# Masked cross attention on one core: one maxima pair in each step, side projections spread over the steps, the sums copied out by ScalarE ahead of the reciprocal

## The reference

```
x = x + L0_xattn(ln(x), ctx)          # cross attention, one head
x = x + L0_attn(ln(x))                # causal self attention, 16 heads
x = x + L0_ffn(ln(x))                 # mixture of 8 experts
x = x + L1_xattn(ln(x), ctx, mask)    # masked cross attention, then self attention, then a gelu layer
x = x + L1_attn(ln(x), key, value)    # quantised self attention
x = x + L1_ffn(ln(x))                 # mixture of 8 experts

# the first part of L1_xattn:
q = split_heads(x @ cq_w + cq_b)      # 16 heads of 8
k = split_heads(ctx @ ck_w + ck_b)
v = split_heads(ctx @ cv_w + cv_b)
scores = einsum('bqhd,bkhd->bhqk', q, k) / sqrt(8) + mask
probs = softmax(scores, axis=-1)      # over the 1601 keys
ca = einsum('bhqk,bkhd->bqhd', probs, v)
```

## Time and profile before

| | |
|---|---|
| median of 3 runs | 1376.42 us (1372.77 to 1376.95) |
| profiled execution | 1376.45 us, its span 1374.6 us |
| PE busy | 1044.6 us (76%) |
| DVE busy | 724.5 us (53%) |
| ACT busy | 489.2 us (36%) |
| POOL busy | 223.0 us (16%) |
| mean granted TensorE clock | 0.881 of full speed |
| masked cross attention | the exponentials begin at 485.2 us, the last starts at 973.1 us |

### The profile page before, as it was taken

The page is one execution under the profiler, slowest core; times in us unless marked ns, Lnnn a source line. Parts: engine busy times, 40 slices in busy tenths (PEclk is TensorE's granted clock), DMA queues, the critical chain, the costliest instruction groups (busy, mean ns, idle before and its releaser), DMA issues.

```text
span 1374.6 us, 22315 instructions
## 1 busy us (share of the span) xinstructions
PE 1044.6 (76%) x9246; PEld 738.4 (54%) x9246; DVE 724.5 (53%) x1194; ACT 489.2 (36%) x633; POOL 223.0 (16%) x202
## 2 busy tenths in 40 slices
PE   3676774998863789999999999998476545729888
PEld 1455453777751356666666666665345323428766
DVE  4234766433443556666666656663376477864121
ACT  0235231222231145555555555555223102403333
POOL 2000423121221001111111111100142004220110
PEclk9899886999995589999999999999888867758999
DMA  8581010010302332222333233320000000010110
GB/s 264 193 342 76 1 43 4 25 45 23 93 0 91 112 117 102 101 100 101 115 132 125 100 109 115 103 73 17 1 1 0 1 0 0 1 31 16 32 37 24
DMA packets 41346, 98.47 MB, mean 72 GB/s; under 512 B 9976, under 2 KB 24960, under 8 KB 41264
## 3 DMA queue, kind: packets, MB, share of 16 engines
q1 hardware_dynamic: 41264, 97.29, 20.9%
HBM read 55.49 MB, written 0.73 MB: 41 GB/s over the span
## 4 chain that ended last, share of the span: by engine, by line
PE 46%; DVE 17%; issue 15%; ACT 11%; POOL 4%; SPq 3%; DMA 3%; DVEq 0%; POOLq 0%
PE PS L262 44%; ACT PT L1084 7%; DVE kl L1475 3%; DVE mx L1492 3%; ACT kh L1071 2%; DVE prT L1481 2%; SPq L893 2%; DVE u_all L275 1%; POOL work_area L390 1%; DMA ctxT<-in_ctx_T 1%; POOL PT L390 1%; DVE x L675 1%; POOL blank_g L257 1%; POOL rstd_all L281 1%; PE PS L292 1%
## 5 line engine op out<-in xcount | busy, mean ns | idle before, releaser
L1492 DVE TENSOR_REDUCE mx<-PS 128x2 f32<-128x1024 f32 x192 | 230.4, 1217 | 74.8 <-PE PS L262 74.6
L1084 ACT ACTIVATE PT<-PS 128x1024 f32<-128x1024 f32 (+1 forms) x208 | 212.4, 1021 | 97.9 <-PE PS L262 97.9
L262 PE MATMUL PS<-QB,KS 128*128 128x256 f32 (+1 forms) x832 | 166.8, 323 | 25.1 <-ACT PT L1084 17.9
L262 PE MATMUL PS<-QB,QS 128*128 128x512 f32 x576 | 159.1, 425 | 24.5 <-DVE wcol L663 22.5
L262 PEld LDWEIGHTS PS<-QB,KS 128*128 128x128 f32 (+1 forms) x832 | 115.7, 187 | 70.2 <-ACT PT L1084 37.6
L262 PEld LDWEIGHTS PS<-QB,QS 128*128 128x128 f32 x576 | 109.7, 201 | 61.5 <-issue 27.6
L262 PE MATMUL PS<-PT,work_area 128*32 128x128 f32 (+1 forms) x3328 | 134.4, 279 | 0.5 <-ACT PT L1084 0.5
L262 PE MATMUL PS<-KS,QB 64*128 64x512 f32 (+1 forms) x512 | 109.7, 459 | 11.5 <-DMA KS<-kl 9.5
L675 DVE SCALAR_TENSOR_TENSOR x<-PS,wcol,x 128x128 f32<-128x128 f32 x128 | 44.9, 350 | 138.1 <-PE PS L262 134.7
L262 PEld LDWEIGHTS PS<-PT,work_area 128*32 128x32 f32 (+1 forms) x3328 | 78.4, 109 | 43.6 <-issue 36.2
L262 PE MATMUL PS<-nat_area,work_area 128*128 128x128 f32 (+2 forms) x928 | 85.0, 275 | 13.7 <-DVE work_area L670 5.9
(11 more groups left out here) (240 smaller groups left out, 1420.1 us busy)
## 6 DMA issues: line engine op xcount, KB each, us to landing
KS<-kh SPq DMA_DIRECT2D x32, 800.5 KB
ctxT<-in_ctx_T SPq DMA_DIRECT2D x24, 800.5 KB, 4.9
nat_area<-in_ctx_tiles SPq DMA_DIRECT2D x16, 832.0 KB, 6.5
KS<-kl SPq DMA_DIRECT2D x16, 800.5 KB
work_area<-in_ctx_T SPq DMA_DIRECT2D x8, 800.5 KB, 10.1
nat_area<-in_L_ffn_experts_w SPq DMA_DIRECT2D x24, 256.0 KB, 3.2
nat_area<-in_L_ffn_W SPq DMA_DIRECT2D x16, 256.0 KB, 3.0
KS<-mask_parts SPq DMA_DIRECT2D x32, 50.1 KB
```

The source lines that it names most:

```text
L262: return T.matmul(o, l, r, start=start, stop=stop, **k)
L1084: P["exp_a"].done(S.activation(PT[0:rows, par, :], PS[0:rows, 1024:2048], ACT.Exp), f"e{k}")
L1492: ins = V.reduce_max(by_pair[:, :, j // 3, j % 3:j % 3 + 1], src, AX)
```

## The change

- **Maxima.** Each of the 13 steps has exactly one maxima item: steps 0 to 9 have m3 to m12 of batch n + 1, steps 10 to 12 have m0 to m2 of batch n + 2. `MAX_STEPS` goes away.
- **Side items.** The key chunks are in steps 0 to 3 (before in 1 to 4), the sum in step 4 (before 5). The value projection is spread by tiles: tiles 0 to 7 two a step over steps 5 to 8, tiles 8 to 11 in step 9, tile 12 in step 11 (before four tiles each in steps 6, 7 and 8 and tile 12 in step 9). ACT empties a group when its last tile is done. nm stays in step 10.
- **Order on PE in a step.** Scores, nm, the maxima item, the side items, then the value product of the step before. DVE takes nm ahead of the step's maxima item.
- **The sum.** ACT copies bank 7 into `rsum`, and DVE takes the reciprocal in place there. PE's wait for bank 7 behind the sum is for ACT's copy (`sum_a`), no longer for the reciprocal (`sum_v`).
- SP's and POOL's programs are not edited.

```diff
+        progress("sum_a", ["sum"])
...
         def maxima(n, k):
-            b = n + 1 if k < 11 else n + 2
-            return [(b, j) for j in MAX_STEPS[k]] if 0 <= b < BATCH else []
+            b, j = (n + 1, k + 3) if k < 10 else (n + 2, k - 10)
+            return [(b, j)] if 0 <= b < BATCH else []
...
+        def value_group(c):
+            return next(g for g, (k0, k) in enumerate(TG) if k0 <= c < k0 + k)
+
+        def sides(n, k):
+
+            return [item for item in SIDES[k]
+                    if 0 <= n + (1 if isinstance(item, int) else SIDE_OF[item[0]]) < BATCH]
+
+        def closed(items):
+
+            out = []
+            for item in items:
+                if not isinstance(item, int):
+                    out.append(item)
+                elif item + 1 == sum(TG[value_group(item)]):
+                    out.append(f"v{value_group(item)}")
+            return out
...
                 if item == "sum":
-                    at(nc.tensor, "sum_v", "sum", b)
+                    at(nc.tensor, "sum_a", "sum", b)
...
             def empty(item, n):
+                if item[0] == "s":
+                    at(S, "sum_p", item, n - 1)
+                    if n >= 2:
+                        at(S, "fin_g", "on", n - 2)
+                    P["sum_a"].done(S.activation(rsum, bank(7, 256), ACT.Copy), item)
...
-                    for b, j in maxima(n, k)[:1]:
+                    items = sides(n, k)
+                    if "nm" in items:
+                        beside("nm", n, k)
+                    for b, j in maxima(n, k):
                         maximum(b, j)
+                    for item in items:
+                        if item != "nm":
+                            beside(item, n, k)
                     if k and 0 <= n < BATCH:
                         values(n, k - 1)
                     if k == 0 and n >= 1:
                         values(n - 1, KT - 1)
-                    for b, j in maxima(n, k)[1:]:
-                        maximum(b, j)
-                    if side(n, k):
-                        beside(k, n)
...
                 elif item == "sum":
-                    at(V, "sum_p", "sum", n - 1)
-                    if n >= 2:
-                        at(V, "fin_g", "on", n - 2)
-                    P["sum_v"].done(V.reciprocal(rsum, bank(7, 256)), "sum")
+                    at(V, "sum_a", "sum", n - 1)
+                    P["sum_v"].done(V.reciprocal(rsum, rsum), "sum")
...
-MAX_STEPS = ([2], [3], [4], [5], [6], [7, 8], [9], [10, 11], [12], [], [], [0], [1])
-SIDES = (None, "k0", "k1", "k2", "k3", "sum", "v0", "v1", "v2", "v3", "nm", None, None)
+SIDES = (("k0",), ("k1",), ("k2",), ("k3",), ("sum",), (0, 1), (2, 3), (4, 5), (6, 7), (8, 9, 10, 11), ("nm",), (12,), ())
```

More of the change, by code:

```diff
@@ L805, in maxima, with bank7_free @@
         def maxima(n, k):
-            b = n + 1 if k < 11 else n + 2
-            return [(b, j) for j in MAX_STEPS[k]] if 0 <= b < BATCH else []
+            b, j = (n + 1, k + 3) if k < 10 else (n + 2, k - 10)
+            return [(b, j)] if 0 <= b < BATCH else []
         SIDE_OF = {"k": 2, "v": 1, "n": 1, "s": -1}
[L812 to L819, removed]
+        def value_group(c):
[11 more added lines that the diff above has]
+            return out
+        def bank7_free(n, k):
+            before = [(m, item) for m in range(-2, n + 1) for i in range(KT) for item in closed(sides(m, i))
+                      if (m, i) < (n, k)]
             if before:
-                m, i = before[-1]
-                item = SIDES[i]
+                m, item = before[-1]
                 b = m + SIDE_OF[item[0]]
                 if item == "sum":
-                    at(nc.tensor, "sum_v", "sum", b)
+                    at(nc.tensor, "sum_a", "sum", b)
                 elif item[0] == "v":
@@ L1089, in slot @@
                         P["acc_a"].done(S.activation(acc_sb, bank(6, 256), ACT.Copy), "acc")
-                    if side(n, k):
-                        empty(SIDES[k], n)
+                    for item in closed(sides(n, k)):
+                        empty(item, n)
             slots(slot)
@@ L1209, in _, with beside @@
                 P["q3_p"].done(mm(bank(h), W["L1_xattn_cq_w"][:, :], xT_all[:, 512 * h:512 * h + 512]), f"q{h}")
-            def beside(k, n):
-                item = SIDES[k]
-                bank7_free(k, n)
+            def beside(item, n, k):
                 if item == "sum":
+                    bank7_free(n, k)
                     at(T, "acc_a", "acc", n - 1)
                     P["sum_p"].done(mm(bank(7, 256), consts[:, C_SEL:C_SEL + 128], acc_sb), "sum")
[L1218 to L1226, removed]
+                elif item == "nm":
+                    bank7_free(n, k)
+                    at(T, "max_v", "nm", n + 1)
+                    P["max_p"].done(T.transpose(bank(7, 128, 8), nm[:, :], ident), "nm")
+                elif isinstance(item, int):
+                    g = value_group(item)
+                    k0, count = TG[g]
+                    if item == k0:
+                        bank7_free(n, k)
+                    rows = 128 if item < FULL else TAIL
+                    o = 3584 + 128 * (item - k0)
+                    last = mm(PS[0:rows, o:o + 128], ctxT[:, (n + 1) % 2, 128 * item:128 * item + rows], W["L1_xattn_cv_w"][:, :])
+                    if item + 1 == k0 + count:
+                        P["vals_p"].done(last, f"v{g}")
+                else:
+                    bank7_free(n, k)
                     c0, cw = CHUNKS[int(item[1])]
@@ L1232, in beside @@
                     P["keys_p"].done(mm(bank(7, cw), W["L1_xattn_ck_w"][:, :], ctxT[:, n % 2, c0:c0 + cw]), item)
-                else:
-                    at(T, "max_v", "nm", n + 1)
-                    P["max_p"].done(T.transpose(bank(7, 128, 8), nm[:, :], ident), "nm")
             def maximum(b, j):
@@ L1501, in slot @@
                 for k in range(KT):
+                    items = closed(sides(n, k))
+                    if "nm" in items:
+                        beside("nm", n)
                     for b, j in maxima(n, k):
                         maximum(b, j)
-                    if side(n, k):
-                        beside(SIDES[k], n)
+                    for item in items:
+                        if item[0] in "ks":
+                            beside(item, n)
             ln_all_vector(3, x, u_all)
```

## The result

The changed kernel takes 1448.03 us (median of 4, 1445.99 to 1451.14) against 1376.56 before: ratio 1.053, interval 1.050 to 1.056. The forecast was slower, 1392 us, with a range up to 1404. The direction and the place were right, the size was not: 71 us lost instead of 16. The profiled execution has a span of 1449.4 us.

The account below looks back on a forecast made before the run. It took a cross-attention slot to be bound by PE's own work (93% busy) plus its waits. Slots and edges +2 and the clock +14 made +16 us on 1376, so 1392 us, range 1368 to 1404.

Parts of the forecast that it names:

- The wait on the reciprocal goes: Step 4: ACT's copy frees bank 7 early, so PE's 1.01 us wait ahead of the first value tiles disappears.
- What is late next: Slot end: later tile 12 delays SP's load and nm copies; next scores start 4.75 us after issue, waiting 2.57 us.
- the lower bound of 4.45: Next slot's scores, order kept: earliest start after the load's issue, 4.4 us for its landing plus 0.05 handover.
- The clock, "13 gaps x 5/7 x 1.5 = +14": Slots 0 to 12: a 2.8 us PE gap each, five of seven lowering the clock, 1.5 us lost each; +14 us.
- the upper bound of twice that: Low-clock stretch behind a gap: at most twice the assumed 3.4 us, costing 3.0 us instead of 1.5.
- "No PE work goes away", the pieces in a new order: Slot steps: PE work unchanged, reordered pieces keep their old start-to-start times, summing to 28.80 us, 2.33 less than before.
- step 11 starts 25.1 us into the slot: Sign of a right forecast: steps 0 to 10 of a slot sum to 25.07 us.
- The edges: Outside slots 1 to 12: slot -1 +1.3, slot 0 +2.1, slot 13 -2.3, slot 14 -2.4, end +0.45 us.
- the clock holds: Rival: the gap ahead of the scores occurs but does not lower the clock; 1378 us, chance 0.2.
- the small copies are not held behind the load: Rival: nml arrives sooner, scores start within 4.3 us of the load's issue; 1364 us, chance 0.12.
- 31.37 as forecast: Length of a steady slot before the clock's cost: 25.07 up to step 11 plus 6.30 to the next slot.
- +16 as forecast: Whole kernel: total predicted loss in us, +2 from slots and edges and +14 from the clock.

Follow-up runs that it names:

- b_copy: Kernel before the change, with only ACT's copy of the sum out of bank 7 and DVE's reciprocal in place added; 1362.3 us, ratio 0.989.
- a_tile12: Changed kernel with value tile 12 in step 9 instead of 11, tiles 4 to 7 in step 7 and 8 to 11 in step 8; 1373.1 us, ratio 1.000.
- a_swap: Changed kernel with SP's two copies of nm issued ahead of the wait for the last value group and of the context load; 1389.7 us, ratio 1.010.
- a_last_fill: a_last with six spare products on PE at the end of step 12 of slots 0 to 12; 1388.4 us, ratio 1.009.
- a_tile12_last: a_tile12 with the side items behind the value product of their step, as before the change; 1341.8 us, ratio 0.975.
- a_fill: Changed kernel with five spare products on PE at the end of step 12 of slots 0 to 12; 1410.1 us, ratio 1.026.
- a_tile12_acc: a_tile12 with ACT's accumulator copy in step 0 moved behind its copy of key chunk k0; 1364.1 us, ratio 0.991.
- a_last: Changed kernel with the side items behind the value product of their step, nothing else; 1415.2 us, ratio 1.029.
- a_acc: Changed kernel with ACT's accumulator copy in step 0 moved behind its copy of key chunk k0; 1435.5 us, ratio 1.045.
- b_order: Kernel before the change, with only PE's undivided side item moved ahead of the value product, in its old step; 1421.5 us, ratio 1.031.

## Why the prediction was wrong

The steps of the prediction, in its order.

- **The wait on the reciprocal goes**: right. b_copy alone gives 14 us.
- **What is late next**: right, in place and size. Slots 1 to 13 wait for nml behind the load. From issue to scores it took 4.28 to 5.21 us, 4.78 in the middle, where 4.75 was taken; the wait is 2.62 us in the slot shown (2.11 to 3.05), where 2.57 was forecast. Moving tile 12 (a_tile12) or SP's two blocks (a_swap) takes it away. In the order of a_last_fill it costs 47 us over a_tile12_last. Only the lower bound of 4.45, the landing of the load and a handover, was too strict. In most slots the scores start 0.4 us after the load has landed, but in slot 7 they start at 741.81, 4.28 us after its issue and 0.1 before it has landed, so the copies do not always wait for its end.
- **The clock, "13 gaps x 5/7 x 1.5 = +14"**: this is the term that was mis-sized. It measured 38 us (changed kernel against a_fill), 3.06 us a slot. Both counts were low. The clock fell around all 13 gaps, not 9. And the low stretch was not 3.4 us: slots 1 to 12 have 97 us at the lower level, 8.1 each. The price per us there was about right: 3.06 / 8.1 = 0.38, as slot 0 had shown (2.7 us for 7.1), where 1.5 for 3.4 was taken. I had taken the length of a stretch from gaps in other stages, four of the five with expert matmuls behind them, and the upper bound of twice that was too low as well.
- **"No PE work goes away", the pieces in a new order**: this step was wrong, and nothing stood for it in the sum or the rivals. I costed the new order of side item and value product at nothing, because each piece was taken as start to start in the old order. The prediction's own sign, that step 11 starts 25.1 us into the slot, shows it: in a_fill, at full clock, it starts 27.4 us in. A float32 item ahead of the value product costs PE 0.2 us more in each of steps 4 to 9 and 0.04 to 0.09 in the key steps, where the loop of bank 7 hides most of it, and with the clock up it makes ACT's accumulator copy hold up kh of k0. Together 31 us at full clock (a_tile12 against a_tile12_last): 9 of it are the copy's (a_tile12_acc), 22 are the rest, most of it the 0.2 us each.
- **The edges**: +3.1 ahead of slot 0 and +2.1 in it (forecast +1.3, +2.1), slot 13 +3.3 (forecast -2.3: it starts at the lower clock behind slot 12's gap and carries the order), slot 14 -1.1 (forecast -2.4), the end +0.4 (forecast +0.45).
- **The rivals**: that the clock holds did not occur. That the small copies are not held behind the load was to show in scores under 4.3 us after its issue; of slots 1 to 13 one is there, by 0.02 us, and the others have 4.58 to 5.21.

With both terms put right a slot comes out: 31.37 as forecast, +2.3 for the order up to step 11 (27.4 against 25.1) and -0.1 from there to the next slot (6.2 against 6.3) make 33.6, where a_fill has 33.61. The fallen clock, by the difference to a_fill, is the 3.06 from there to 36.67. Over the whole kernel, +16 as forecast, +24 more for the clock (38 for 14) and +31 for the order make +71, which is what was measured. The 31 are from a_tile12 and a_tile12_last, without the wait, so this is an estimate and not a division that is exact: with the wait there and the clock held, the order is worth 22 us (a_fill against a_last_fill), since it also sets when the load is issued; and in the old order the clock is worth 27 (a_last against a_last_fill).

Open: why most low stretches last 10.2 us. They go with when the clock falls, as said at a_acc, but no run set that by itself. The cost of a change of shape on PE is read from the starts of the products in all these traces; what holds the next product back was not tried.

## What to carry to other kernels

When an item moves, follow every queue that waits for it: here one 0.2 us tile moved two steps later held up a transfer, two 4 KB copies behind it, and the next slot's start. A gap on PE of 2 us and more is not priced by its own length. Count the time at the lower clock that follows it, in the same stage, and if the gap cannot go, spare products in it can pay for themselves, as the five of a_fill did (38 us). And a duration read start to start belongs to the pair of neighbours: after a reordering it has to be read anew.

## What the runs showed of the hardware

- The clock fell around every one of the 13 gaps of 2.1 to 3.1 us in the changed kernel, and around 9 of 14 gaps of 1.9 us in b_order, each amid PE work that was otherwise dense. It held around one of 2.71 us in a_acc, and around two of seven of 2.7 to 2.9 us in the kernel before. In the changed kernel it came back after 3.4, 6.8 or 10.2 us, though PE had no wait from the end of the gap on.
- Two products on PE that use the array alike follow each other closely: 0.03 us from the start of the last value tile to the start of the scores. Where the shape changes (`128*128`, `64*128`, `128*32`) the next product starts 0.20 us after the last one of 128 columns.
- In the changed kernel two 4 KB copies issued 0.4 and 1.1 us behind an 800 KB load on the same queue let PE start 4.28 to 5.21 us after the load's issue, mostly 0.4 us after the load had landed and once 0.1 before.
- A reciprocal of 128x256 takes 1.74 us from SBUF and 1.75 from PSUM.
